# A cross-attention and routed-FFN block on one core: weight products turned by DMAs inside SBUF in place of PE transposes

## What is computed

```
q = LN(x) Wq / 8;  k = ctx Wk;  v = ctx Wv
s = einsum(bqhd, bkhd -> bhqk);  s = einsum(bhqk, hi -> biqk, Wth1)
p = softmax(s over k);  p = einsum(bhqk, hi -> biqk, Wth2)
x = x + einsum(p, v) Wo
assignment: for each expert in turn, the 256 best rows not yet taken
x = x + routed back (rows + gelu(LN(rows) w1[e] + b1[e]) w2[e] + b2[e])
```

## Time and profile before

| what | value |
|---|---|
| median of 3 runs | 313.31 us |
| profiled execution | 312.71 us on the device, span of its instructions 310.9 us |
| PE / DVE / POOL / ACT busy | 292.0 / 229.5 / 194.7 / 153.4 us |
| granted PE clock, mean | 0.994 of full |
| DMA | 37.79 MB, mean 122 GB/s |
| chain that ended last | PE 78%, DVE 10%, POOL 5% of the span |

### The profile page before, as it was taken

The page is one execution under the profiler, slowest core; times in us unless marked ns, Lnnn a source line. Parts: engine busy times, 40 slices in busy tenths (PEclk is TensorE's granted clock), DMA queues, the critical chain, the costliest instruction groups (busy, mean ns, idle before and its releaser), DMA issues.

```text
span 310.9 us, 6807 instructions
## 1 busy us (share of the span) xinstructions
PE 292.0 (94%) x2149; PEld 252.9 (81%) x2151; DVE 229.5 (74%) x801; ACT 153.4 (49%) x282; POOL 194.7 (63%) x246
## 2 busy tenths in 40 slices
PE   8999998999999999999997779999999999998990
PEld 3999897999999999999872239898989888888990
DVE  0669999888878888888877877767676767338450
ACT  1357646355555555554554225363636353577720
POOL 8200334467878787787733445768787878859831
PEclk9999999999999999999999999999999999999997
DMA  7995002971000000001101321554656565624110
GB/s 256 353 375 197 3 0 79 382 250 35 36 34 34 34 34 34 34 34 67 38 34 70 136 67 36 174 167 179 198 181 198 190 196 177 209 62 143 53 65 19
DMA packets 21769, 37.79 MB, mean 122 GB/s; under 512 B 2416, under 2 KB 14960, under 8 KB 21360
## 3 DMA queue, kind: packets, MB, share of 16 engines
q1 hardware_dynamic: 19184, 31.16, 28.9%
q0 software_dynamic: 2560, 6.31, 6.6%
HBM read 31.17 MB, written 6.29 MB: 120 GB/s over the span
## 4 chain that ended last, share of the span: by engine, by line
PE 78%; DVE 10%; POOL 5%; issue 3%; ACT 2%; ACTq 0%; POOLq 0%; DVEq 0%
PE pair L1178 68%; PE pair L1254 4%; PE pair L1228 2%; DVE cmpb L994 2%; POOL w1p L508 2%; POOL out_dram L529 2%; PE pair L1266 1%; PE pair L1422 1%; DVE sm L851 1%; DVE wneg L765 1%; DVE pair L1028 1%; POOL G L498 1%; DVE ok L1011 1%; POOL pr L278 0%; POOL yT L514 0%
## 5 line engine op out<-in xcount | busy, mean ns | idle before, releaser
L1178 PE MATMUL pair<-yT,w1p 128*128 128x256 f32 x384 | 54.0, 290 | 0.3 <-POOL yT L514 0.3
L1178 PE MATMUL pair<-Bm,pT 128*128 (+1 forms) x384 | 50.4, 287 | 0.2 <-ACT pT L603 0.2
L1178 PEld LDWEIGHTS pair<-yT,w1p 128*128 128x128 f32 x384 | 48.4, 190 | 1.2 <-POOL yT L514 0.5
L1178 PE MATMUL pair<-Am,xTp 128*128 (+1 forms) x192 | 48.3, 400 | 0.0
L1178 PEld LDWEIGHTS pair<-Bm,pT 128*128 128x128 f32 x384 | 47.1, 191 | 0.4 <-issue 0.4
L1178 PE MATMUL pair<-w2s,hT 128*128 128x256 f32 x192 | 47.1, 389 | 0.0
L278 POOL TENSOR_TENSOR pr<-pr,rs 128x1024 f32<-128x1024 f32 (+1 forms) x16 | 31.3, 1954 | 24.4 <-DVE rs L858 15.3
L508 POOL TENSOR_TENSOR w1p<-w1s,w1p 128x512 fp32r<-128x512 f32 x32 | 40.0, 1273 | 5.4 <-ACT w1p L669 5.3
L1178 PEld LDWEIGHTS pair<-Am,xTp 128*128 128x128 f32 x192 | 34.9, 188 | 7.0
L1178 PEld LDWEIGHTS pair<-w2s,hT 128*128 128x128 f32 x192 | 33.8, 190 | 4.3
L714 ACT ACTIVATE hT<-pair,b1s 128x256 f32<-128x256 f32 x48 | 20.2, 471 | 33.8 <-PE pair L1178 33.8
(11 more groups left out here) (153 smaller groups left out, 573.5 us busy)
## 6 DMA issues: line engine op xcount, KB each, us to landing
w1s<-w_dram SPq DMA_DIRECT2D x8, 1024.0 KB, 5.3
w2s<-w_dram SPq DMA_DIRECT2D x8, 1024.0 KB, 5.9
rows_scratch<-row SPq DMA_DIRECT2D x16, 256.0 KB, 2.0
xs<-x_dram SPq DMA_DIRECT2D x1, 2048.0 KB, 17.2
xTs<-xT_dram SPq DMA_DIRECT2D x1, 2048.0 KB, 18.9
wk_s<-wk_dram SPq DMA_DIRECT2D x1, 1024.0 KB, 5.3
wv_s<-wv_dram SPq DMA_DIRECT2D x1, 1024.0 KB, 7.5
wqT_s<-wqT_dram SPq DMA_DIRECT2D x2, 512.0 KB, 9.0
```

Of the source, the lines that this page charges most:

```text
L1178: return nc.tensor.matmul(out_, l, r, start=start, stop=stop)
```

## The change

The products keep contexts on partitions: kvT becomes the stationary operand and the weights the moving one, 256 columns at a time, so AB is [context, head, channel]. Each group of 8 contexts is then copied by one DMA from 8 partitions of 16 KB to 128 partitions of 1 KB, 16 DMAs for each side, on SP's queue; four of them share a semaphore. The transposes and their copies are gone, and mix is laid out for the new order (context outside, head inside). x and xT are loaded in halves, with the small inputs and the first half of xT ahead of the regrouping of side 0, the first half of x ahead of that of side 1. The statistics of the first half of x stand between the mixed remainders, those of the second in steps 2 to 4; the second root (POOL) goes to step 5, and the loop is unrolled to step 7. The tiles ctx_s to wo_s change their order in memory. For the first expert, matmuls of the first and third block that need only the rounded rows go ahead (round 7 and gap 8), the second block goes ahead of the next search's transposes and the fourth behind them; half of its remainder is made by DVE; and ACT writes the rounded rows of every expert ahead of the full ones.

```diff
-            AB = sb("AB", [P, 2, CC, GROUPS, H, K8], f32, prep)
+            AB = sb("AB", [P, 2, H, C], f32, prep)
-        A_FIRST, A_LOOP, A_LOOP_END, A_LAST = -1, 5, 15, T + 4
+        A_FIRST, A_LOOP, A_LOOP_END, A_LAST = -1, 7, 15, T + 4
-        MIXED, LATE, FILLS = 36, 44, 52
+        MIXED, LATE, FILLS = 20, 28, 36
-                last = copy(AB[:, side, cc, :, h:h + 7:2, :].rearrange("p g h k -> p h g k"),
-                            src[:].rearrange("p (h g k) -> p h g k", h=4, g=GROUPS), 1.0)
-            else:
-                side, g = (f - 20) // 8, (f - 20) % 8
-                last = copy(ABT[:, side, 2 * g:2 * g + 2, :], src[:].rearrange("p (g c) -> p g c", g=2), 1.0)
+                side, n = (f - 4) // 8, (f - 4) % 8
+                h = n // 2 * 4 + n % 2
+                last = copy(AB[:, side, h:h + 3:2, :], src.rearrange("p (h c) -> p h c", h=2), 1.0)
...
-            sp.dma_start(xs[:], x.rearrange("(t p) c -> p t c", p=P)).then_inc(s_in["x"], 16)
-            sp.dma_start(xTs[:], xT.rearrange("(c p) n -> p c n", p=P)).then_inc(s_in["xT"], 16)
+            def regroup(side):
+                wait_copied(sp, 11 + 8 * side)
+                for g in range(GROUPS):
+                    sp.dma_start(ABT[:, side, g, :], AB[g * K8:(g + 1) * K8, side]).then_inc(s_group[side][g // 4], 16)
...
             sp.dma_start(dig[:], digits.unsqueeze(0).to_broadcast([P, 2, FIRST])).then_inc(s_in["dig"], 16)
+            load_xT(0)
+            regroup(0)
+            load_x(0)
+            regroup(1)
+            load_x(1)
+            load_xT(1)
...
-                if isinstance(s, int) and s in (-1, 0):
-                    x_root(s + 1)
+                if isinstance(s, int) and s in (-1, 5):
+                    x_root(0 if s < 0 else 1)
+                if isinstance(s, int) and s == 5:
+                    pool.wait_ge(s_in["xT1"], 16)
...
             def y_rest(e, v):
-                for c in range(CC):
-                    pool.wait_ge(e_yT, 4 * e + 2 * c + 2)
+                for c in range(CC if e > 0 else 1):
+                    pool.wait_ge(e_yT, 4 * e + CC + c + 1)
...
-                for c in range(CC):
-                    for to in (yF[:, c, :], yT[:, 0, v, c, :]):
+                for to in (yT[:, 0, v], yF):
+                    for c in range(CC):
...
-                if 21 <= f < MIXED and f % 2 == 1:
-                    x_stats((f - 21) // 2)
-                if f == MIXED - 1:
-                    x_variance(0)
                 if MIXED <= f < MIXED + T // 2:
-                    x_stats(T // 2 + f - MIXED)
-            x_variance(1)
+                    x_stats(f - MIXED)
+            x_variance(0)
...
+                    if isinstance(s, int) and s == 0:
+                        for quad in range(4):
+                            dve.wait_ge(s_group[1][quad], 4 * 16)
                     nc.vector.tensor_tensor(pr[:, v, :].rearrange("p (g i k) -> p g i k", i=H, k=K8),
...
+                    for n in {2: (8, 9), 3: (10, 11, 12), 4: (13, 14, 15)}.get(s, ()):
+                        x_stats(n)
+                    if s == 4:
+                        x_variance(1)
...
+            def first_rows_rest():
+                c = CC - 1
+                dve.wait_ge(e_yT, CC + c + 1)
+                nc.vector.tensor_tensor(yT[:, 1, 0, c, :], yF[:, c, :], yT[:, 0, 0, c, :].bitcast(f32),
+                                        ALU.subtract).then_inc(e_yD, 1)
...
+                if u == 0:
+                    first_rows_rest()
                 if searches(k):
                     select(k)
...
-                            last = mm(bank[(f + m // 4 * 2 + o) % 8][:, m % 4 * P:(m % 4 + 1) * P],
-                                      w[q, m, c * P:(c + 1) * P], kvT[q, side, m, :], True, True)
+                        last = mm(bank[(f + o) % 8][:, m % 2 * C:(m % 2 + 1) * C], kvT[q, side, m, :], w[q, m, :], True, True)
...
-            for side in range(2):
-                for g in range(8):
-                    wait_copied(pe, max(f - 8, 11 + 8 * side))
-                    for h in range(2):
-                        for c in range(CC):
-                            last = nc.tensor.transpose(bank[f % 8][:, h * C + c * P:h * C + (c + 1) * P],
-                                                       AB[:, side, c, 2 * g + h, :, :].rearrange("p h k -> p (h k)"), ident)
-                    last.then_inc(s_fill, 1)
-                    f += 1
...
-                wait_copied(pe, max(bank_before(f), 27 + 8 * side))
+                wait_copied(pe, bank_before(f))
+                pe.wait_ge(s_group[side][g // 4 * 2 + g % 2 if side == 0 else g // 2], 4 * 16)
...
                     expert_part(k, r)
+                    if u == 0 and r == 7:
+                        up_rounded(u, 0)
...
                 expert_part(k, 8)
+                if u == 0:
+                    up_rounded(u, 2)
+                    up_rest(u, 0)
+                    up_rest(u, 2)
...
                 expert_part(k, 9)
+                if u == 0:
+                    up(u, 1)
...
+                    if u == 0:
+                        up(u, 3)
```

More of the change, by code:

```diff
@@ L165, in build @@
         w1p = sb("w1p", [P, 2, 2, CC, F], f32r)
-        s_in = {n: sem("in_" + n) for n in ("cst", "ctx", "wk", "wv", "wq0", "wq1", "wo", "rep", "small", "x", "xT", "b2", "dig")}
+        s_in = {n: sem("in_" + n) for n in ("cst", "ctx", "wk", "wv", "wq0", "wq1", "wo", "rep", "small", "x0", "x1", "xT0", "xT1", "b2", "dig")}
+        s_group = [[sem(f"side{side}_groups{quad}") for quad in range(4)] for side in range(2)]
         s_consts, s_ones, s_mix = sem("consts_made"), sem("ones_made"), sem("mix_made")
@@ L772, in x_stats @@
             def x_stats(t):
-                dve.wait_ge(s_in["x"], 16)
+                dve.wait_ge(s_in["x0" if t < T // 2 else "x1"], 16)
                 nc.vector.bn_stats(bst[:, t, :], xs[:, t, :]).then_inc(s_bn1, 1)
@@ L1207, in _ @@
                 wait_copied(pe, 1 + 2 * side)
[L1208 to L1231 removed]
+                for m in range(HD // P):
+                    if side == 0 and m % 4 == 0:
+                        pe.wait_ge(s_wcA, m // 2 + 2)
+                        pe.wait_ge(s_wcD, m // 2 + 2)
+                    if m % 2 == 0 and f >= 8:
+                        wait_copied(pe, f - 7)
+                    for o in range(2):
+                        q = slice(o * D, (o + 1) * D)
+                        last = mm(bank[(f + o) % 8][:, m % 2 * C:(m % 2 + 1) * C], kvT[q, side, m, :], w[q, m, :], True, True)
+                    if m % 2 == 1:
+                        last.then_inc(s_fill, 2)
+                        f += 2
+            pe.wait_ge(s_in["cst"], 16)
             pe.wait_ge(s_mix, 4)
@@ L1435, in up, with up_rounded, up_rest @@
                         pe.wait_ge(e_hs, FC * (e - 1) + 2 * (g + 3))
-                to = bank[1 + g % 2][:, q * CAP:(q + 1) * CAP]
+            def up_rounded(e, f):
                 if f == 0:
[L1439 to L1443, removed]
-                        pe.wait_ge(e_yl, CC * e + c + 1)
-                        mm(to, w1p[:, 0, v, c, 0:P], yT[:, 1, v, c, :], False, c == CC - 1)
+                    pe.wait_ge(e_w1l, W1_PARTS * (e + 1))
+                up_free(e, f)
+                v, q = e % 2, slice(f * P, (f + 1) * P)
+                for c in range(CC):
+                    pe.wait_ge(e_yT, 4 * e + c + 1)
+                    for i in range(2):
+                        mm(up_bank(f), w1p[:, i, v, c, q], yT[:, 0, v, c, :], c == 0 and i == 0, False)
+            def up_rest(e, f):
+                v, q = e % 2, slice(f * P, (f + 1) * P)
+                for c in range(CC):
+                    if e == 0 and c == CC - 1:
+                        pe.wait_ge(e_yD, 1)
+                    else:
+                        pe.wait_ge(e_yl, CC * e + c + (1 if e == 0 else 0))
+                    mm(up_bank(f), w1p[:, 0, v, c, q], yT[:, 1, v, c, :], False, c == CC - 1)
+            def up(e, f):
+                if f == 0:
+                    up_rounded(e, f)
+                    up_rest(e, f)
                     return
+                v, q = e % 2, slice(f * P, (f + 1) * P)
+                up_free(e, f)
                 for c in range(CC):
-                    last = mm3(to, lambda i: w1p[:, i, v, c, f * P:(f + 1) * P], lambda i: yT[:, i, v, c, :], c == 0,
-                               c == CC - 1)
-                if q == 1:
+                    last = mm3(up_bank(f), lambda i: w1p[:, i, v, c, q], lambda i: yT[:, i, v, c, :], c == 0, c == CC - 1)
+                if f % 2 == 1:
                     last.then_inc(e_h, 1)
@@ L1485, in expert_part @@
                 if 0 <= e < E:
-                    for f in range(*UP_REST[first_part(e)].get(gap, (0, 0))):
+                    rest = UP_REST[first_part(e)] if e > 0 else {1: (4, 6), 2: (6, 8)}
+                    for f in range(*rest.get(gap, (0, 0))):
                         up(e, f)
@@ L1491, in expert_part @@
```

(6 more changed lines are left out.)

46 lines of the change are left out of this document (27 added, 19 removed).

## The result

| | before | after |
|---|---|---|
| median | 313.2 us (312.8 to 313.4) | 343.4 us (342.5 to 344.5) |
| ratio | 1 | 1.097 (95%: 1.095 to 1.099) |
| span of the profiled execution | 310.9 us | 341.7 us |

A forecast was written before the change was run, and what follows sets the result against it. PE, with DVE second, was taken to bound the kernel up to the attention loop. 312.71 + 2.2 (later loop) - 0.2 (first expert) = 314.7 us profiled, 315.3 on the median; own range 314 to 318, wider range 309 to 326.

The forecast's parts named there:

- What bounds the kernel: Up to the attention loop: PE has almost no idle time from 14 us, DVE is second; both must get earlier.
- Products: Products with Wq and Wo ahead of the regrouping: 16 paired matmuls of 256 columns, 3.4 us a side.
- What the regrouping costs: The 32 DMAs replacing the transposes: 0.43 us of transfer and 0.48 of SP issue per 128 KB.
- Reads from few partitions are slow: Rival on the regrouping DMAs: about 331 us at 1.1 us each, 364 at 2.2; chance 0.13.
- Half the transfer engines: Rival on the regrouping: 8 partitions use half the engines, 0.62 to 0.86 us per DMA, 318 to 325 us; chance 0.13.
- PE after that: Mixed fills after the products: PE waits 6.1 us for side 1; logits of tile 0 start 0.4 us later before clock cost.
- the clock: During PE's wait for side 1 the clock falls, slowing side 1's four fills: 2.0 us taken, 0 to 3.3 possible.
- the price taken: Regrouping DMAs priced at 0.43 us of transfer and 0.48 of issue per 128 KB, between lower and upper ends.
- Is met: DVE's new wait for all of side 1 (38.5) before tile 0's subtraction is met, as the maximum comes at 41.9.
- Statistics of the second half of x: Eight statistics, 3.4 us of DVE, moved into idle time of steps 2 to 4: cost 0, bound 1.
- second root: Second root on GpSimd moves into its idle time in step 5: cost 0.
- First expert: Second block goes ahead of the next search's transposes; the next total comes 0.2 us earlier, no more.

The follow-up runs named there:

- the last version: Against the kernel before: side 0 regrouped by DMA from partitions four apart, side 1 transposed on PE, with copy layout, transpose order and GpSimd's root mended; 310.7 us, ratio 0.993.
- The run with two heads a DMA: Against the changed kernel: each regrouping DMA reads two heads of all 128 contexts, 16 DMAs of 256 KB in place of 32 of 128 KB; 316.3 us.

## Why the prediction was wrong

The forecast was 315.3 us, its range ended at 326, and the time is 343.4.

- **What bounds the kernel:** right. PE and DVE both had to come earlier, and the last version gains where both do.
- **Products:** 3.56 us for Wq (14.14 to 17.70) and 3.62 for Wo against my 3.4 a side; in pairs, as I took them.
- **What the regrouping costs: this step failed.** "I take 0.43 and 0.48: same pieces, same stretch" took its price from xs, whose 1 KB pieces are right but which comes from HBM into 128 partitions. A DMA out of 8 neighbouring partitions takes 1.47 us, three times that. In the place of one limit there are three: about half of the transfer engines' time with 8 partitions, how those partitions lie, and 0.66 us of SP for each DMA. Even the last alone is above my 0.48. Nor was 0.48 the pace of a full queue: the earlier trace rows have SP held for 3.29 and 6.63 us by xs and xTs.
- **The rival was the case.** "Reads from few partitions are slow" gave 331 at 1.1 us and 364 at 2.2; a straight line between them gives 342 at 1.47. It had 0.13. It named the wait before the subtraction, which is there, but stands behind others: without it only 3.9 us come back. "Half the transfer engines" was right as well, but as a lower bound: its 0.62 to 0.86 us is what contexts four apart show (0.81), at 324.9 us, where it gave 318 to 325. I had taken two mechanisms for alternatives, and both act on the same DMA. I gave them little weight because "nothing here speaks for or against"; that was no reason to take the cheap end.
- **PE after that, and the clock:** near at the price taken, in part by luck. The run with two heads a DMA lands the first half of x for the first statistic at 31.63 (I had 31.5), starts logits of tile 0 at 39.65 (38.8), loses 1.6 us on side 1's fills (2.0) and ends at 316.3 (315.3). But its PE waits 2.76, 1.50 and 2.54 us, and not 6.1 in one place ahead of the fifth fill; and the clock is low from the first of these waits on (0.53 from 24 to 28), so side 0's fills take 6.53 us against 3.74 in the earlier trace rows, which I had at full speed. In the changed kernel a lower clock at side 1's fills is hidden: the maximum is ready 4.55 us ahead of the subtraction.
- **A wait that I did not see:** DVE's order has one statistic of x behind every mixed remainder, so x, which is queued between the two sides, stops the remainders, and with them PE's banks: 14.39 us ahead of the fill at 53.88. Here the next fill waits 2.19 us for a DMA all the same.
- **"Is met", of the wait before the subtraction:** it was not, and it is worth 3.9 us of the 30.2, as its removal shows. It comes from memory, not from data.
- **Statistics of the second half of x, second root:** 0, right. DVE is busy 38.55 us in place of 35.87 in six steps, and their length stays.
- **First expert:** 0.2 faster predicted, 0.6 slower measured. The comparison that the total waits for was seen; that ScalarE's new order delays GpSimd's remainder for all experts was not; that this delay is the whole loss is not shown.

## What to carry to other kernels

Price a DMA inside SBUF by its source: how many partitions it reads, how they lie, and SP's time for each DMA. Rows of loads from HBM into 128 partitions did not give the price of a narrow source; a narrow destination was not tried. Where no row shows the source, give the dear end the chance that the mechanisms deserve. Regroup by DMA only what other work covers: half of it, from partitions four apart, under PE's own transposes of the other half, made this kernel 0.7% faster, while all of it made it 9.7% slower from neighbouring partitions, and still 1.3% from partitions four apart in the order of first use.

## What was not expected of the hardware

Eight partitions four apart move 161 GB/s where eight neighbours move 87, at the same bytes, pieces and count. SP takes 0.66 us for a DMA of 128 pieces of 1 KB out of 128 partitions, and 0.68 for one with twice the pieces. Two queues raised the rate from 161 to 214 GB/s and the time by 3 us.
